# An attention layer and a routed feed-forward on one core: expert groups whose two 128-row blocks each have an expert of their own

## The reference

```python
# x, ctx: 64 batches x 128 rows x 256 columns, f32; 8 experts, hidden size 512, 2 experts a token
x = x + xattn(layernorm(x), ctx, ctx)      # softmax over the batch axis
h = layernorm(x)                           # 8192 tokens x 256
logits = einsum('th,eh->te', h, router_w)
topk_logits, topk_idx = top_k(logits, 2);  probs = softmax(topk_logits)
hmid = gelu(einsum('th,efh->etf', h, w1) + b1[:, None, :])
y    = einsum('etf,ehf->eth', hmid, w2) + b2[:, None, :]
x = x + sum over the token's two experts of probs * y
```

## Time and profile before

| | us |
|---|---|
| median of 3 runs | 859.92 |
| the runs | 860.61, 854.1, 859.92 |
| span of the profiled execution, first to last instruction | 909.8 |
| busy: TensorE / weight loads / VectorE / ScalarE / GpSimd | 770.1 / 649.5 / 622.8 / 390.1 / 574.0 |
| mean granted TensorE clock, share of full speed | 0.927 |

### The profile page before, as it was taken

How to read it: one execution, slowest core, us unless ns; L and a number is a source line. 1 busy time by engine, 2 the same in 40 slices (tenths; PEclk the granted TensorE clock), 3 DMA queues, 4 the chain that set the end, 5 groups by cost and what they waited for, 6 DMA issues and landing times. The chain is left out here.

```text
span 909.8 us, 22499 instructions
## 1 busy us (share of the span) xinstructions
PE 770.1 (85%) x5931; PEld 649.5 (71%) x5932; DVE 622.8 (68%) x1520; ACT 390.1 (43%) x715; POOL 574.0 (63%) x815
## 2 busy tenths in 40 slices
PE   6999996999996449888989887989588889879886
PEld 5678885878885338766877776978367778767775
DVE  6998999899998758655655654363465656556554
ACT  3555664576666204333333433143133333334331
POOL 5664776788884056666576566366766666665663
PEclk9999997999997559999999999799789999999998
DMA  7887773488885124444344443343533343333330
GB/s 227 251 250 240 237 228 114 137 269 266 267 275 192 53 60 134 131 147 157 118 148 156 142 133 119 112 140 76 159 106 111 106 129 108 97 115 116 96 107 2
DMA packets 82200, 137.20 MB, mean 151 GB/s; under 512 B 10075, under 2 KB 55140, under 8 KB 82032
## 3 DMA queue, kind: packets, MB, share of 16 engines
q0 software_dynamic: 23104, 68.43, 24.9%
q1 hardware_dynamic: 59056, 68.26, 23.9%
HBM read 94.56 MB, written 47.59 MB: 156 GB/s over the span
## 5 line engine op out<-in xcount | busy, mean ns | idle before, releaser
L680 PE MATMUL psum<-work,w1T_high 128*128 128x256 f16 x1248 | 227.4, 285 | 53.5 <-ACT work L1067 36.6
L1059 ACT ACTIVATE work<-psum,slots 128x256 f32<-128x256 f32 x312 | 130.2, 471 | 309.4 <-PE psum L680 233.0
L703 PE MATMUL psum<-w2T_high,slots 128*128 x1248 | 214.7, 277 | 6.2 <-issue 5.1
L680 PEld LDWEIGHTS psum<-work,w1T_high 128*128 x1248 | 124.0, 102 | 85.9 <-issue 67.2
L680 PE MATMUL psum<-work,w1T_low 128*128 128x256 f16 x624 | 177.6, 285 | 3.5 <-issue 3.5
L703 PE MATMUL psum<-w2T_low,slots 128*128 x624 | 172.4, 276 | 1.7 <-issue 1.7
L952 DVE CAST slots<-work 128x512 f16<-128x512 f32 x156 | 71.0, 455 | 138.4 <-ACT work L1059 114.8
L703 PEld LDWEIGHTS psum<-w2T_high,slots 128*128 128x128 f16 x1248 | 119.6, 99 | 23.2 <-issue 9.2
L561 PE MATMUL psum<-slots,work 128*128 (+1 forms) x512 | 124.0, 392 | 7.4 <-ACT slots L991 6.8
L540 POOL DMA_INDIRECT rows_second<-slots x78 | 82.3, 1055 | 66.0 <-issue 35.6
L968 DVE SCALAR_TENSOR_TENSOR slots<-psum,slots 128x256 f32<-128x256 f32 x156 | 68.2, 478 | 78.5 <-remote 63.9
(11 more groups left out here) (126 smaller groups left out, 1125.2 us busy)
## 6 DMA issues: line engine op xcount, KB each, us to landing
work<-in_ctx SPq DMA_DIRECT2D x96, 256.0 KB, 3.5
rows_first<-slots SPq DMA_DIRECT2D x32, 514.0 KB, 3.9
slots<-in_x SPq DMA_DIRECT2D x32, 256.0 KB, 3.8
work<-in_L_ffn_w SPq DMA_DIRECT2D x32, 256.0 KB, 3.2
work<-in_x SPq DMA_DIRECT2D x32, 256.0 KB, 3.1
slots<-rows_first,slots POOLq DMA_INDIRECT x86
rows_second<-slots POOLq DMA_INDIRECT x78
slots<-rows_second,slots POOLq DMA_INDIRECT x78
```

The source lines that it names most:

```text
L680: mm = pe.matmul(h, w1T[pw][:, f, c, bass.ds(e * P, P)], xT[r2][:, (px * HC + c) * GROUP:(px * HC + c + 1) * GROUP], start=(c == 0 and px ...
L703: mm = pe.matmul(y, act16[r2][pa][:, f * GROUP + s * P:f * GROUP + (s + 1) * P], w2T[pw][:, f, bass.ds(e * DIM, DIM)], start=(f == 0 and p ...
L1059: last = act.activation(act32[r2][:, f * GROUP:(f + 1) * GROUP], psum[:, 2 + 2 * r2 + f // 2, (f % 2) * GROUP:(f % 2 + 1) * GROUP], ACT.Ge ...
```

## The change

A group is still two blocks of 128 rows, but each expert's list is padded to whole blocks and not to whole groups, and each block of a group has its own expert. A round has 64 + 7 = 71 blocks at most, in 36 groups; 72 groups in all. The owner table has one expert per block, packed in pairs (8 x first + second); `experts_of` loads such a pair into a register and splits it. The first layer runs each f for both halves with 128 columns each, the second takes the weights of its half. ScalarE reads the bias from the table of all biases by a register address, with one activation per half, and loads the pair itself; `ring_b1`, `x_b1` and GpSimd's expert load are dropped. GpSimd copies the next group's indices at the end of a step. The listing of the second round moves to step 30 and 18 steps, not 12, are written out around the change of rounds.

```diff
-GROUPS = TOKENS // GROUP + EXPERTS - 1
+GROUPS = (TOKENS // P + EXPERTS - 1 + SUB - 1) // SUB
@@ expert_steps
-    whole = GROUPS // LANES
-    resume = -(-(GROUPS + L_G2) // LANES)
+    whole = GROUPS // LANES - 1
+    resume = -(-(GROUPS + 2 * L_G2) // LANES)
...
-        LIST_STEP = GROUPS // LANES * LANES
+        LIST_STEP = (GROUPS // LANES - 1) * LANES
+
+        def experts_of(eng, g):
+
+            both = eng.value_load(owners_i[0:1, bass.ds(g, 1)], min_val=0, max_val=EXPERTS * EXPERTS - 1)
+            return [eng.snap((both >> 3).with_bounds(min_val=0, max_val=EXPERTS - 1)), eng.snap(both & (EXPERTS - 1))]
@@ gpsimd
-            pool.wait_ge(r_owner, 1)
             pool.wait_ge(r_index, 1)
 
+            def indices_of(g, r):
+
+                pool.tensor_copy(ring_idx[:, r * 4:r * 4 + 4], index[:, bass.ds(g * 4, 4)]).then_inc(x_idx, 1)
+
+            indices_of(0, 0)
+
             def group(i, k, n, rnd):
-                if is_step(i, k, GROUPS):
-                    pool.wait_ge(r_index, 2)
...
-                    after(pool, x_out[r], n * 32 + k // LANES * 32)
-                    pool.tensor_copy(ring_idx[:, r * 4:r * 4 + 4], index[:, bass.ds(g * 4, 4)]).then_inc(x_idx, 1)
-                    pool.wait_ge(x_idx, 1)
-                    e = pool.value_load(owner_i[0:1, bass.ds(g, 1)], min_val=0, max_val=EXPERTS - 1)
-                    pool.tensor_copy(ring_b1[:, r * FC:(r + 1) * FC], b1T[:].rearrange("p e f -> p (e f)")[:, bass.ds(e * FC, FC)]).then_inc(x_b1, 1)
                     wait_apart(pool, x_idx, g + 1)
...
+                if live(i, k, -1, ALL):
+
+                    if is_step(i, k, GROUPS - 1):
+                        pool.wait_ge(r_index, 2)
+                    after(pool, x_out[(k + 1) % LANES], n * 32 + (k + 1) // LANES * 32)
+                    indices_of(i + k + 1, (k + 1) % LANES)
@@ tensor
-                    e = pe.value_load(owner_i[0:1, bass.ds(g, 1)], min_val=0, max_val=EXPERTS - 1)
+                    owners = experts_of(pe, g)
                     pe.wait_ge(x_xT, g + 1)
                     after(pe, x_act, g * 2 - 2)
                     for f in range(FC):
-                        h = psum[:, 2 + 2 * r2 + f // 2, (f % 2) * GROUP:(f % 2 + 1) * GROUP]
-                        for c in range(HC):
-                            for px, pw in ((0, 0), (1, 0), (0, 1)):
-                                mm = pe.matmul(h, w1T[pw][:, f, c, bass.ds(e * P, P)], xT[r2][:, (px * HC + c) * GROUP:(px * HC + c + 1) * GROUP],
-                                               start=(c == 0 and px == 0 and pw == 0), stop=(c == HC - 1 and pw == 1))
+                        for s, e in enumerate(owners):
+                            h = psum[:, 2 + 2 * r2 + f // 2, (f % 2) * GROUP + s * P:(f % 2) * GROUP + (s + 1) * P]
+                            for c in range(HC):
+                                for px, pw in ((0, 0), (1, 0), (0, 1)):
+                                    mm = pe.matmul(h, w1T[pw][:, f, c, bass.ds(e * P, P)], xT[r2][:, ((px * HC + c) * SUB + s) * P:((px * HC + c) * SUB + s + 1) * P],
+                                                   start=(c == 0 and px == 0 and pw == 0), stop=(c == HC - 1 and pw == 1))
...
-                    e = pe.value_load(owner_i[0:1, bass.ds(g, 1)], min_val=0, max_val=EXPERTS - 1)
+                    owners = experts_of(pe, g)
                     pe.wait_ge(x_low, g * 2 + 2)
                     after(pe, x_sum, g - 1)
-                    for s in range(SUB):
+                    for s, e in enumerate(owners):
@@ vector
-            chain(dve.tensor_scalar(count_i, psum[:, 3, 0:16], float(GROUP - 1), None, ALU.add))
+            chain(dve.tensor_scalar(count_i, psum[:, 3, 0:16], float(P - 1), None, ALU.add))
...
+            chain(*[dve.tensor_tensor(pst[:, r], ends[0:1, r * 8:r * 8 + 8].unsqueeze(1).to_broadcast([1, TILES, EXPERTS]),
+                                      iota_n[:].unsqueeze(2).to_broadcast([1, TILES, EXPERTS]), ALU.is_le) for r in range(ROUNDS)])
             chain(dve.tensor_reduce(owner, past.rearrange("p (n e) -> p n e", e=EXPERTS), AX_X, ALU.add))
-            dve.tensor_scalar(owner_i, owner, float(EXPERTS - 1), None, ALU.min).then_inc(r_owner, 1)
+            chain(dve.tensor_scalar(owner, owner, float(EXPERTS - 1), None, ALU.min))
+            by_pair = owner.rearrange("p (n s) -> p n s", s=SUB)
+            dve.scalar_tensor_tensor(owners_i.unsqueeze(2), by_pair[:, :, 0:1], float(EXPERTS), by_pair[:, :, 1:2], ALU.mult, ALU.add).then_inc(r_owner, 1)
...
-                e = dve.value_load(owner_i[0:1, bass.ds(g, 1)], min_val=0, max_val=EXPERTS - 1)
+                owners = experts_of(dve, g)
@@ scalar
+            act.wait_ge(r_owner, 1)
...
-                    act.wait_ge(x_b1, g + 1)
+                    owners = experts_of(act, g)
...
-                        last = act.activation(act32[r2][:, f * GROUP:(f + 1) * GROUP], psum[:, 2 + 2 * r2 + f // 2, (f % 2) * GROUP:(f % 2 + 1) * GROUP],
-                                              ACT.Gelu, bias=ring_b1[:, r * FC + f:r * FC + f + 1], scale=1.0 / WSCALE)
+                        for s, e in enumerate(owners):
+                            at = (f % 2) * GROUP + s * P
+                            last = act.activation(act32[r2][:, f * GROUP + s * P:f * GROUP + (s + 1) * P], psum[:, 2 + 2 * r2 + f // 2, at:at + P],
+                                                  ACT.Gelu, bias=b1T[:].rearrange("p e f -> p (e f)")[:, bass.ds(e * FC + f, 1)], scale=1.0 / WSCALE)
```

More of the change, by code:

```diff
@@ L174, in xattn_ffn @@
         iota_e = sb("iota_e", [P, EXPERTS])
-        iota_g = sb("iota_g", [1, GROUPS])
+        iota_n = sb("iota_n", [1, TILES])
         mark = sb("mark", [P, BATCH], F16)
@@ L315, in xattn_ffn @@
         empty = take(TILES)
[L316 to L319, removed]
+        index = take((ROUNDS * GROUPS + 1) * 2 * SUB).bitcast(I32)
+        past = take(ROUNDS * TILES * EXPERTS, 1)
+        owner = take(ROUNDS * TILES, 1)
+        owners_i = take(ROUNDS * GROUPS, 1).bitcast(I32)
         ring_idx = take(LANES * 2 * SUB).bitcast(I32)
-        ring_b1 = take(LANES * FC)
         assert taken[0] <= 28 * 2 * ROW
@@ L337, in xattn_ffn @@
         x_idx = sem("x_idx")
-        x_b1 = sem("x_b1")
         x_tr = sem("x_tr")
@@ L469, in _ @@
             pool.iota(iota_e[:], [[1, EXPERTS]], base=0, channel_multiplier=0, allow_small_or_imprecise_dtypes=True)
-            pool.iota(iota_g[:], [[GROUP, GROUPS]], base=0, channel_multiplier=0, allow_small_or_imprecise_dtypes=True)
+            pool.iota(iota_n[:], [[P, TILES]], base=0, channel_multiplier=0, allow_small_or_imprecise_dtypes=True)
             pool.iota(mark[:], [[0, 4], [ROWS, BATCH // 4]], base=1, channel_multiplier=1, allow_small_or_imprecise_dtypes=True)
@@ L859, in _ @@
             dve.wait_ge(r_pos, 1)
-            chain(dve.tensor_scalar(count_i, psum[:, 3, 0:16], float(GROUP - 1), None, ALU.add))
-            chain(dve.tensor_scalar(count_i, count_i, GROUP.bit_length() - 1, None, ALU.arith_shift_right))
-            chain(dve.tensor_scalar(blocks, count_i, float(GROUP), None, ALU.mult))
+            chain(dve.tensor_scalar(count_i, psum[:, 3, 0:16], float(P - 1), None, ALU.add))
+            chain(dve.tensor_scalar(count_i, count_i, P.bit_length() - 1, None, ALU.arith_shift_right))
+            chain(dve.tensor_scalar(blocks, count_i, float(P), None, ALU.mult))
             blk = blocks.rearrange("p (r e) -> p r e", r=ROUNDS)
@@ L909, in indices @@
                 chain(dve.tensor_reduce(token, listed.rearrange("p (q n) -> p n q", q=4), AX_X, ALU.add))
-                ix = index.rearrange("p (r n w s) -> p r n w s", r=ROUNDS, w=2, s=SUB)[:, rnd]
+                ix = index[:, 0:ROUNDS * GROUPS * 2 * SUB].rearrange("p (r n w s) -> p r n w s", r=ROUNDS, w=2, s=SUB)[:, rnd]
                 chain(dve.tensor_scalar(empty, token, 0.0, float(SKIPPED), ALU.is_equal, ALU.mult),
@@ L922, in _ @@
                 hot_lanes(dve, 0, q)
-            pst = past.rearrange("p (r g e) -> p r g e", r=ROUNDS, e=EXPERTS)
-            chain(*[dve.tensor_tensor(pst[:, r], ends[0:1, r * 8:r * 8 + 8].unsqueeze(1).to_broadcast([1, GROUPS, EXPERTS]),
-                                      iota_g[:].unsqueeze(2).to_broadcast([1, GROUPS, EXPERTS]), ALU.is_le) for r in range(ROUNDS)])
+            pst = past.rearrange("p (r n e) -> p r n e", r=ROUNDS, e=EXPERTS)
+            chain(*[dve.tensor_tensor(pst[:, r], ends[0:1, r * 8:r * 8 + 8].unsqueeze(1).to_broadcast([1, TILES, EXPERTS]),
+                                      iota_n[:].unsqueeze(2).to_broadcast([1, TILES, EXPERTS]), ALU.is_le) for r in range(ROUNDS)])
             chain(dve.tensor_reduce(owner, past.rearrange("p (n e) -> p n e", e=EXPERTS), AX_X, ALU.add))
-            dve.tensor_scalar(owner_i, owner, float(EXPERTS - 1), None, ALU.min).then_inc(r_owner, 1)
+            chain(dve.tensor_scalar(owner, owner, float(EXPERTS - 1), None, ALU.min))
```

(2 more changed lines are left out.)

## The result

The kernel before took 860.26 us (median of four runs, 854.1 to 861.17), the changed one 941.88 us (four runs, 940.0 to 944.73). The ratio is 1.096, 95% interval 1.093 to 1.099: 82 us slower. The forecast was 940 us.

What follows compares the result with a forecast made beforehand. GpSimd paces before; then TensorE's sequencer binds at 8.3 us: 71 steps 589, first 5, last 3, listing 9, change of rounds 8, together 614 against 514, so 960 us. Between that and 907 it said 940, range 885 to 990.

Steps and rivals of the forecast that it cites:

- The distances count, not the durations: TensorE's sequencer: an address pair costs its 0.24 us spacing, not the 0.078 us recorded as work.
- Eight more pairs in the first layer: TensorE's sequencer, first layer: 16 blocks in place of 8 need 8 more address pairs, +1.9 us a step.
- Unpacking: Shift and mask at the two expert loads a step on TensorE's sequencer: +0.4 us, bounds 0 and 0.8.
- The starting step of 5.3 us: Sequencer's step in the kernel before, read as 5.3 us against the array's 5.69, hidden by 0.4 us.
- Narrow pairs: First layer: a load and matmul of 128 columns takes 0.06 us, half a wide one; 48 take 2.6 to 3.0 us.
- GpSimd, 5.8 us a step: GpSimd without its expert's bias copy: step falls from 6.04 to 5.8 us, covered by the sequencer's 8.3, worth nothing.
- The same place: GpSimd's index copy, moved behind the previous step's scatters, still stands between last scatter and next gather.
- The faster rival: Sequencer stays hidden, GpSimd paces 72 steps of 6.2 us: 807 us, chance 0.15.
- Change of rounds: Between the two rounds gathers wait for all scatters: 8 us added to the stage.
- slowdown over everything: Alternative reading of the profile's extra 50 us: everything, sequencer included, shrinks by 860/910, giving 907 us.
- The 50 us of before's profile: Profiled span 909.8 us against median 859.9: taken as mostly stretches where TensorE stops with work queued.
- The rival in which it falls in the first layer: TensorE's clock drops under dense narrow matmuls in a third of the steps: +65 us, 1,005 us, chance 0.07.

Runs made afterwards that it cites:

- e3: Kernel before, wide matmuls and 78 groups kept, but the expert in two unpacked registers, so more address operations in both layers; 934.86 us, ratio 1.087.
- e4: Changed kernel with the weights' high table also in place of the low one (wrong product), so three matmuls share one address; 812.23 us, ratio 0.944.
- e6: Changed kernel with GpSimd's index copy moved ahead of the scatters; 944.43 us, ratio 1.097.
- e7: Kernel before with two expert registers in the second layer alone, plus the unpacking; 859.22 us, ratio 0.998.
- e2: Kernel before with the first layer's matmuls cut to 128 columns, same expert register and number of address pairs; 859.89 us, ratio 1.001.
- e1: Changed kernel without its new groups: 78 groups of one expert, bias read by register, indices copied at step end; 855.75 us, ratio 0.993.
- e5: e1 with GpSimd's index copy moved ahead of the two scatters; 817.38 us, ratio 0.949.
- e8: e4 with GpSimd's index copy moved ahead of the scatters, as in e5; 796.63 us, ratio 0.926.

## Why the prediction was right, point by point

**The bound.** TensorE's sequencer was hidden before and binds now: right. e3 gives the cost with the array's work unchanged, e4 takes it away with the array's work unchanged, with ScalarE's narrow activations and all new waits still in place, and e6 shows that GpSimd no longer matters. "The distances count, not the durations" was right: 0.078 us recorded a pair, 0.24 us paid. The Trainium skill ("Perfetto Trace Analysis", Sequencer-only Instruction) has the record hold execution alone; e3's 75 us agree with that.

**Terms of the step.** Eight more pairs in the first layer, +1.9 us: 16 now take 4.07 us on the chain, 3.73 for 15. Four more in the second, +1.0: counts as forecast, 0.24 us each in e7. Unpacking +0.4: one ALU_OP more and a longer FUSED_REGOPS a load, 0.3 to 0.4 by the distances. The starting step of 5.3 us was 0.2 to 0.6 too long (e7), and I had taken off 0.3 for other reasons that no run isolates; the two largely cancel, which is luck. 8.3 us was said; 8.06 is the median, and 8.11 the mean without the listing's step.

**A term that was missing.** At each of the 8 turns of the hardware loops, every sixth step, the step is 8.7 to 9.0 us, mostly 8.95. That is up to 0.9 us more, some 7 us over the stage. The operations of the turn itself take 0.56 us of it (from 759.23 to the next load at 759.79); in e3 and e7 the same step is longer by 0.4 to 0.5 us only. Before, it lay in the slack.

**Narrow pairs** at 0.055 us: right (e2). **ScalarE, VectorE** covered: right, with 8 activations of 0.37 us and the copy of 1.04, 4.0 us a step.

**GpSimd, 5.8 us a step:** wrong, and harmless for this sum. It is 6.3 us in e1 and 6.2 in e4, since the gap runs from the last copy that the gather reads. "The same place" for the moved copy was right as GpSimd's order goes, but in e5 the place costs 38 us. The faster rival counted with 6.2 us a step and had 807 us; with the sequencer hidden e4 gives 6.2 and 812.

**Listing,** 9 us: the step that holds it takes 17.99 us, 9.9 more. **Change of rounds,** 8 us: wrong. Three of the steps there show nothing of it in the chain, and no step from 578.88 to 707.07 us is over 8.08 us:
```profile
642.91 2.79 PE psum L711 x24
...
650.87 2.79 PE psum L711 x24
...
658.92 2.79 PE psum L711 x24
```
The gathers wait for the last scatters, but with 8 us a step and four groups in flight they are still early enough. A slower pace covers waits that a faster one shows. In the changed kernel VectorE waits for such a gather at most 6.6 us at a time, and TensorE does not feel it; in e8, at 5.8 us a step, VectorE waits up to 11.6 us and TensorE up to 7.0, and three steps there take 13.7, 8.8 and 8.5 us.

**The sum, and luck.** Stage 614 forecast and 601 found. The 71 full steps took 8.18 us each and not 8.3, 8 us less; the change of rounds took nothing, 8 less; the first step, with no L703, took 7.7 and not 5, 3 more; the listing 1 more. With 333.5 us ahead and 8.2 behind the stage that is 942.9, where the sum had 960. The forecast of 940 came closer than its own sum, because 20 us had been taken off for a slowdown over everything that turned out not to exist. The mechanism and the way of the change were right; that the number fell within 2 us was luck.

**The 50 us of before's profile.** I took them to be stretches of that one execution. No later profile has them: the changed kernel's span is 942.9 against 944.7 us for the same run, e2's 853.7 against 855.5, with the step at a mean of 6.46 us against 7.17 in the profile of before, and no chain of a later profile has a share of an unknown queue. The granted clock was also at its lower level for longer there, 54 us of the stage behind its head against 17 in e2, often just behind such a stretch (from 746.8 to 750.2 us behind the one at 742.47). How much each is worth, and what caused them, is open. The alternative, a slowdown over everything and 907 us, is out: the distances of the address pairs are the same 0.24 us in that profile and in those without the stretches.

**The clock.** The rival in which it falls in the first layer is out. Two stretches of the changed kernel (us; busy us of TensorE, its loads, VectorE, ScalarE, GpSimd; granted clock; DMA share; GB/s), the first in the listing:
```profile
564.00:574.00 10.00, 10.00 (x67) 10.00 (x66) 0.66 (x2) 0.00 (x0) 4.21 (x5) 0.70 0.42 130
590.00:650.00 60.00, 56.49 (x608) 42.83 (x607) 29.34 (x58) 23.49 (x67) 33.22 (x38) 1.00 0.38 120
```
In the narrow matmuls it stays at the upper level, 2.4 GHz, from 346.0 us to the listing and again from 578.1 to 940.0 us. At the lower, 1.2 GHz, it is from 567.9 to 578.1 us, in and just behind the listing, as before, and at the head of the stage, until 339.2 us and from 342.6 to 346.0, while TensorE still waits between its first groups. In the profile of before the head's stretch ended at 340.6 us.

**The other side.** The faster rival had its condition right: sequencer hidden gives 812 (e4) or 797 us (e8). It needed fewer operations a block, and the change as written does not have that. e4 and e8 show what this would be worth, not a kernel that has it.

## What to carry to other kernels

Where matmuls take their address from a register, count the sequencer's operations in a step beside the array's columns, by the distance between them. Each new register, and each table addressed with it, has its own address to work out. Splitting wide matmuls costs nothing while the halves share a register (e2); a register for each half doubles the addresses and halves the work that hides each. And a run whose time does not move can still have changed its bound (e7). Put a small copy whose result an indirect DMA reads ahead of other DMAs and not right before its reader.

## What the runs showed of the hardware

- On TensorE's sequencer a FUSED_REGOPS is followed by the next operation after 0.124 us and an ALU_OP after 0.112 us, in the medians of before, e2, e7 and the changed kernel alike, whether the array is covered or waits. Recorded are 0.046 and 0.032.
- From a copy on GpSimd to an indirect DMA that reads it 0.84 or 1.08 us pass; between two DMAs 0.30 us; from the copy to a DMA that does not read it 0.17 us.
- The step with a turn of the hardware loop was 0.9 us longer in the changed kernel and 0.4 to 0.5 in e3 and e7, all bound by TensorE's sequencer. In e5, bound by the array, every step at a turn takes 5.69 us like the others.
- The medians of the kernel before lie between 859.8 and 860.3 us in four sets of runs, and single runs of one kernel spread by up to 1.4% (e2), yet one profiled execution was 50 us longer than the median, with TensorE standing still in places that no other profile has.
